# Causal masking of diagonal score blocks: from an addition on VectorE to an accumulated matmul

## The chip, the cores and the metric

The kernel runs on one core of one Trainium2 chip. The metric is the time of one execution on the device in microseconds (us). Where engines are named, PE is TensorE, DVE is VectorE, ACT is ScalarE, POOL is GpSimd and SP is SyncE.

## The reference

Input X is 4 sequences of 2048 tokens with 256 channels, in float32. Four residual blocks follow one another, each after a layer norm: attention A, a feed-forward block with token shift, attention B, and the same feed-forward block again. Cut to the attention, which is what the change touches:

```
# block A: 16 heads of 16 channels
scores = einsum('bhqk,bhsk->bhqs', q, k) * scale
scores = where(tril(ones(S, S)), scores, -inf)      # key s <= query q
attn_out = einsum('bhqs,bhsk->bhqk', softmax(scores), v)

# block B: 16 heads of 16 channels; q is k moved by one token, k and v are normalised
att = einsum('bhqd,bhkd->bhqk', q, k)
att = where(t[None, :] <= t[:T - 1, None], att, -inf)
y = einsum('bhqk,bhkd->bhqd', softmax(att), v)      # row 0 is zero

x = x + A(ln(x));  x = x + ffn(ln(x));  x = x + B(ln(x));  x = x + ffn(ln(x))
```

## The kernel before

**Stages.** A loop over the 4 sequences runs, for each, the projections of block A, `attend("A")`, a feed-forward stage, the projections of block B, `attend("B")` and the second feed-forward stage. So there are 8 attentions. Each engine has its own program, and the programs meet at semaphores.

**An attention.** The 16 heads are taken 4 at a time (`HG`), so an attention has 4 instances, and the whole kernel 32. They run in a loop of two passes (`Fori(0, NHG // 2)`); each pass holds two instances that are written out, `u` = 0 and `u` = 1. There are thus three places in an attention where one instance follows another: `u` 0 to 1 in the first pass, the loop's jump back (`u` 1 to 0), and `u` 0 to 1 in the second pass. Where an instance begins, `begin` (line 898) reads flags and, where a head's scores could be large, runs `row_maxima`; otherwise it branches past that code.

**Banks and groups.** Scores are computed transposed, with 128 keys on the partitions and up to 512 queries on the free axis. A unit is one key block of 128 against one query chunk of 512 (or the part of the chunk that isn't masked wholly) for one head. `score_banks` (line 68) packs units into banks of 512 columns. Query chunk `qc` has 4*`qc` key blocks ahead of the diagonal, each a full bank for each of the 4 heads, and then the diagonal blocks: block `d` with 512 columns, `d+1` with 384 and `d+3` with 128 in one bank, two heads' `d+2` with 256 each in one bank. `GROUPS` pairs the banks; an instance has 69 groups, and 21 of them are diagonal (6 in the first chunk, 5 in each of the other three). A diagonal bank holds one or two units, and the first 128 columns of each unit are the block in which the triangular mask falls. Counted over an instance these are 16 units for each chunk, 64 in all.

**The pipeline.** PE computes the scores of group `gi + 3` (line 932, bf16, 99 contraction rows) and then the value products of group `gi` (line 950, float32). ACT takes the exponential of a group, 1024 columns in one instruction (line 661), from PSUM into `probs` in SBUF. PSUM has three score buffers of two banks (`NS_BUF`), so the scores of group `gi + 3` wait for the exponential of group `gi`; there are six buffers of `probs`. On diagonal groups DVE first adds the mask tile `mask_kq` in PSUM (`masks`, line 1344), 128 columns for each unit, one instruction for each group, and ACT waits for that (`masked`) and not for the scores.

**What else DVE does there.** DVE works through its own program in order: the masks of the chunk's groups, then `take` (line 1360, it copies a finished output chunk out of PSUM), `normalise` (line 1366), and the next chunk's masks. At an instance's end it runs the first three masks of the next instance (`ahead`, line 1382), then `take` of the last chunk, then the jump back where the loop turns, and then the other masks of chunk 0. In the last instance of an attention `first_residual` (line 1309), with a layer norm, stands ahead of the masks of chunk 3. PE's `turn` (line 956) transposes what `take` copied.

**Other names.** `row_maxima` on PE (line 830) already holds an accumulated matmul of `ident_b` and a mask tile (line 846), for query-major scores. `probs` names a semaphore as well as the tile: it counts exponentials. `stage` holds the keys and queries, in bf16 parts, that lines 932 and 843 read.

Of the kernel before, what the change touches and what calls it, by code (L numbers as in the profile page):

```python
# [28 lines left out]
ALU = mybir.AluOpType  # L29
AX_X = mybir.AxisListType.X  # L30

P = 128
# [4 lines left out]
CH = 512  # L37
NCH = S // CH
TB = CH // P
HG = 4  # L40
NHG = H // HG
# [42 lines left out]
GB = 2  # L84
NS_BUF = 3
# [3 lines left out]
GROUPS = [BANKS[0:1], BANKS[1:2]] + [BANKS[i:i + GB] for i in range(2, len(BANKS), GB)]  # L89
NG = len(GROUPS)  # L90
# [61 lines left out]
def hybrid_kernel(nc, t, out):  # L152
    with ExitStack() as ctx:
# [183 lines left out]
        for a in "AB":  # L337
            att[a] = {n: sem(f"{n}_{a}") for n in (
                "kq0", "kq1", *(f"kq_first{c}" for c in range(NCH)), "scores", "probs", "p_free", "vst",
                "masked", "o_ev", "o_T", "o_free", "o_step", "mx_scores", "mx_used", "mx_col", "mx_T", "mx_step", "mx_row",  # L340
                "mx_dma")}

        def held(eng):
# [262 lines left out]
        def _(act):  # L606
# [41 lines left out]
            def attend(a, b, g, left_used):  # L648
                sm = att[a]
                for u in range(2):  # L650
                    inst = b * NHG + g * 2 + u
                    for gi, grp in enumerate(GROUPS):
                        if u == 0 and gi == NP_BUF - 2:
                            act.wait_ge(*left_used)
                        if gi in DIAG_GROUPS:
                            act.wait_ge(sm["masked"], inst * ND + DIAG_GROUPS.index(gi) + 1)
                        else:
                            act.wait_ge(sm["scores"], inst * NG + gi + 1)
                        act.wait_ge(sm["p_free"], P_FREE_0 + inst * NG + gi + 1 - NP_BUF)
                        w = len(grp) * CH  # L660
                        nc.scalar.activation(  # L661
                            probs[:, (u * NG + gi) % NP_BUF, 0:w],
                            ps[:, GB * (gi % NS_BUF):GB * (gi % NS_BUF) + len(grp), :].rearrange("p a n -> p (a n)"),
                            ACT.Exp, scale=SCALE[a]).then_inc(sm["probs"], 1)
                        if u == 1 and gi - 2 in FIRST_O + FIRST_LN:
                            with act.If(g > NHG // 2 - 2):
                                first_copy(b, "AB".index(a), gi - 2)
# [107 lines left out]
        def _(pe):  # L775
# [116 lines left out]
            def attend(a, b):  # L892
# [29 lines left out]
                def scores(u, inst, gi, fresh=False):  # L922
                    kk = stage[0:KROWS, 2 * u, :].rearrange("r (j n) -> r j n", j=HG)
                    qq = stage[0:KROWS, 2 * u + 1, :].rearrange("r (j n) -> r j n", j=HG)
                    if not fresh:
                        pe.wait_ge(sm["probs"], inst * NG + gi + 1 - NS_BUF)
                    if u == 0 and GROUPS[gi][0][0][0] != GROUPS[gi - 1][0][0][0] and gi:
                        first_there(GROUPS[gi][0][0][0])
                    for n, bk in enumerate(GROUPS[gi]):
                        for qc, kb, j, q0, w, col in bk:  # L930
                            o = ps[:, GB * (gi % NS_BUF) + n, col:col + w]
                            last = pe.matmul(o, kk[:, j, kb * P:(kb + 1) * P],  # L932
                                             qq[:, j, qc * CH + q0:qc * CH + q0 + w], start=True, stop=True)
                    last.then_inc(sm["scores"], 1)

                def products(u, inst, gi):
# [250 lines left out]
        def _(dve):  # L1187
# [86 lines left out]
            with dve.Fori(0, B) as b:  # L1274
# [46 lines left out]
                def attend(a):  # L1321
# [19 lines left out]
                            dve.sem_inc(sm["mx_step"], 3 * HG)  # L1341
                            dve.sem_inc(sm["mx_row"], HG)

                    def masks(hg, groups):

                        inst = b * NHG + hg
                        for gi, at, n in groups:
                            dve.wait_ge(sm["scores"], inst * NG + gi + 1)
                            bk = GB * (gi % NS_BUF)
                            nb = len(GROUPS[gi])  # L1350
                            units = ps[:, bk:bk + nb, :]
                            if n == 1:
                                units = units[:, :, 0:P]
                                mask = mask_kq[a][:, :].unsqueeze(1).to_broadcast([P, nb, P])
                            else:
                                units = units.rearrange("p b (n w) -> p b n w", w=P)[:, :, 0:at // P + 1:at // P, :]
                                mask = mask_kq[a][:, :].unsqueeze(1).unsqueeze(1).to_broadcast([P, nb, n, P])
                            nc.vector.tensor_tensor(units, units, mask, ALU.add).then_inc(sm["masked"], 1)  # L1358

                    def take(hg, qc):  # L1360
                        inst = b * NHG + hg

# [19 lines left out]
                    def ahead(hg):  # L1382

                        begin(hg)
                        masks(hg, DIAG[0][:NS_BUF])

                    ahead(0)
                    with dve.Fori(0, NHG // 2) as g:
                        for u in range(2):
                            hg = g * 2 + u  # L1390
                            masks(hg, DIAG[0][NS_BUF:])
                            if u == 1:
                                normalise(hg - 1, NCH - 1)
                            else:
# [2 lines left out]
                            for qc in range(NCH - 1):  # L1397
                                take(hg, qc)
                                normalise(hg, qc)
                                if u == 1 and qc == NCH - 2:  # L1400
                                    with dve.If(g > NHG // 2 - 2):
                                        first_residual("AB".index(a))
                                masks(hg, DIAG[qc + 1])

                            if u == 0:
                                ahead(hg + 1)
# [213 lines left out]
```

## Time and profile before

| | |
|---|---|
| Time, median of 3 runs | 3817.01 us |
| Lowest and highest run | 3812.78 and 3830.15 us |
| Span of the profiled execution, first to last instruction | 3815.5 us |
| PE busy | 3341.0 us, 88% of the span |
| ACT busy | 2521.1 us, 66% |
| DVE busy | 1584.7 us, 42% |
| Mean granted TensorE clock | 0.923 of full speed |
| Exponentials (line 661) | 2208 of 1019 ns |
| Mask additions (line 1358) | 672 in all, 369.3 us busy |

The profiled execution has no time of its own in the profile beside its span; the span is 1.5 us under the median of the runs. Busy time of a PE matmul is modelled from its start to its estimated end and overlaps the next one, so where matmuls follow each other their starts are what tells the pace.

### The profile page before, as it was taken

The numbers are of one execution on the slowest core, as the hardware profiler recorded it, in microseconds if no ns is written. First come the engines' busy times: TensorE is split into PE (matmuls) and PEld (weight loads), VectorE is DVE, ScalarE is ACT, GpSimd is POOL, SyncE is SP. The second block draws the span as 40 slices with busy tenths as digits, with TensorE's granted clock in tenths as the row PEclk, the third lists the DMA queues.
The fourth block names the chain that finished last, engine by engine and source line by source line (L and its number), as shares of the span: only waits on it lengthen the run. The fifth ranks groups of instructions, "written<-read, shape, count | busy, mean of one in ns | idle before, by whom it ended". The sixth has DMA issues, their size and how long they took to land.

```text
span 3815.5 us, 60575 instructions
## 1 busy us (share of the span) xinstructions
PE 3341.0 (88%) x19930; PEld 1358.3 (36%) x19931; DVE 1584.7 (42%) x3607; ACT 2521.1 (66%) x2786; POOL 380.6 (10%) x384
## 2 busy tenths in 40 slices
PE   6999859989899985998989998599898999959988
PEld 4222532225422353222542236222263223622225
DVE  4222682235522278223552227722464212862146
ACT  4888348865488834886459882588636887258853
POOL 4000130001200013000120001300012000120001
PEclk8999979989899997998999999799899999979989
DMA  5420024200432002320053200332015220042200
GB/s 146 74 38 2 1 62 76 36 2 24 129 65 37 2 1 73 65 36 2 23 138 56 36 2 1 87 51 36 2 33 148 36 36 2 1 101 37 36 2 23
DMA packets 96168, 167.82 MB, mean 44 GB/s; under 512 B 10442, under 2 KB 90826, under 8 KB 90826
## 3 DMA queue, kind: packets, MB, share of 16 engines
q1 hardware_dynamic: 95632, 161.14, 19.6%
q8 instruction: 279, 4.57, 0.5%
q14 instruction: 257, 2.11, 0.2%
HBM read 114.82 MB, written 46.24 MB: 42 GB/s over the span
## 4 chain that ended last, share of the span: by engine, by line
PE 70%; DVE 16%; issue 9%; ACT 3%; POOL 1%; DMA 1%; SPq 1%; DVEq 0%; ACTq 0%; POOLq 0%
PE ps L950 29%; PE ps L932 28%; PE ps L826 4%; PE ps L818 3%; PE ps L960 2%; PE ps L803 2%; ACT probs L661 1%; DVE nw_u L1217 1%; DVE nw_u L1219 1%; DVE stage L1421 1%; DVE nw_y L1221 1%; DVE ln_st L1227 1%; DVE stage L1239 1%; DVE pmax L1292 1%; PE ps L868 1%
## 5 line engine op out<-in xcount | busy, mean ns | idle before, releaser
L661 ACT ACTIVATE probs<-ps 128x1024 f32<-128x1024 f32 (+1 forms) x2208 | 2083.7, 1019 | 469.8 <-DVE ps L1358 378.0
L932 PE MATMUL ps<-stage 99*128 99x512 bf16 (+3 forms) x5120 | 1206.9, 362 | 139.9 <-issue 104.4
L950 PE MATMUL ps<-probs,v_st 128*32 128x512 f32 (+3 forms) x10240 | 1215.0, 556 | 4.6 <-issue 4.6
L932 PEld LDWEIGHTS ps<-stage 99*128 99x128 bf16 x5120 | 407.1, 100 | 1150.0 <-ACT probs L661 593.3
L950 PEld LDWEIGHTS ps<-probs,v_st 128*32 128x32 f32 x10240 | 222.3, 111 | 517.7 <-issue 264.6
L1358 DVE TENSOR_TENSOR ps<-ps,mask_kq_B 128x512 f32<-128x512 f32 (+2 forms) x336 | 184.4, 570 | 525.7 <-PE ps L932 522.6
L1358 DVE TENSOR_TENSOR ps<-ps,mask_kq_A 128x512 f32<-128x512 f32 (+2 forms) x336 | 184.9, 570 | 523.4 <-PE ps L932 519.3
L818 PE MATMUL ps<-stage,wT 128*128 128x512 f32 x512 | 233.4, 606 | 12.3 <-DVE stage L1462 7.7
L826 PE MATMUL ps<-wT,stage 128*128 128x256 f32 x1024 | 235.2, 385 | 2.7 <-DVE x_res L1450 2.7
L1364 DVE COPY o_ev<-ps 128x512 f32<-128x512 f32 x128 | 88.5, 692 | 339.2 <-PE ps L950 339.2
L555 POOL TENSOR_TENSOR stage<-xnT 128x512 f32<-128x512 f32 x64 | 65.0, 1037 | 1530.2 <-ACT xnT L646 1327.6
L826 PEld LDWEIGHTS ps<-wT,stage 128*128 128x128 f32 x1024 | 196.6, 194 | 44.3 <-issue 19.7
L1371 DVE TENSOR_SCALAR den<-ps 128x16 f32<-128x16 f32 x128 | 22.4, 175 | 401.5 <-PE ps L960 401.5
L709 ACT ACTIVATE stage<-ps 128x1024 f32<-128x1024 f32 x32 | 32.7, 1023 | 230.1 <-PE ps L818 230.1
L542 POOL COPY v_st<-v_all 128x256 f32 x128 | 45.2, 400 | 1242.8 <-PE ps L950 1240.2
L818 PEld LDWEIGHTS ps<-stage,wT 128*128 128x128 f32 x512 | 98.0, 195 | 123.6 <-issue 104.3
L621 ACT COPY stage<-ps 128x1024 f32<-128x1024 f32 x48 | 48.7, 1014 | 131.5 <-PE ps L818 117.5
L818 PE MATMUL ps<-xnT,wT 128*128 128x512 f32 x256 | 118.1, 615 | 4.4 <-ACT xnT L621 4.4
L1462 DVE SCALAR_TENSOR_TENSOR stage<-stage,mu,xnT 128x512 f32<-128x512 f32 x64 | 63.3, 1027 | 80.8 <-POOL stage L555 80.8
L1227 DVE BATCH_NORM_STATS2 ln_st<-x_res 128x6 f32<-128x256 f32 x256 | 89.7, 412 | 15.8 <-DMA x_res<-in_L_attn_a_X 13.5
L803 PE MATMUL ps<-ident,stage 128*128 128x128 f32 x320 | 48.9, 302 | 53.8 <-DVE stage L1239 52.6
L826 PE MATMUL ps<-wT,probs 128*128 128x256 f32 x384 | 88.1, 383 | 6.5 <-ACT probs L621 6.5
(154 smaller groups left out, 2501.5 us busy)
## 6 DMA issues: line engine op xcount, KB each, us to landing
stage<-part_a SPq DMA_DIRECT2D x36, 512.0 KB
stage<-part_b SPq DMA_DIRECT2D x36, 512.0 KB
part_a<-probs SPq DMA_DIRECT2D x96, 128.0 KB
part_a<-last_parts SPq DMA_DIRECT2D x96, 128.0 KB
stage<-part_a SPq DMA_DIRECT2D x12, 768.0 KB
stage<-part_a SPq DMA_DIRECT2D x36, 256.0 KB
stage<-part_b SPq DMA_DIRECT2D x12, 768.0 KB
stage<-part_b SPq DMA_DIRECT2D x36, 256.0 KB
```

The source lines that it names most:

```text
L555: pool.tensor_tensor(x_diff[:, kt, :], now[:, kt, :], before[:, kt, :], ALU.subtract).then_inc(s_diff, 1)
L661: nc.scalar.activation(probs[:, (u * NG + gi) % NP_BUF, 0:w], ps[:, GB * (gi % NS_BUF):GB * (gi % NS_BUF) + len(grp), :].rearrange("p a n ...
L803: last = pe.transpose(ps[:, bk + kt, tb * P:(tb + 1) * P], src[:, tb, kt * P:(kt + 1) * P], ident[:, :])
L818: last = pe.matmul(ps[:, bk, :], wT[:, w, kt, m * P:(m + 1) * P], src[:, kt, :], start=(kt == 0), stop=(kt == KT - 1))
L826: last = pe.matmul(tok_bank(bk, tb), src[:, kt, tb * P:(tb + 1) * P], wT[:, w, kt, :], start=(kt == 0), stop=(kt == KT - 1))
L932: last = pe.matmul(o, kk[:, j, kb * P:(kb + 1) * P], qq[:, j, qc * CH + q0:qc * CH + q0 + w], start=True, stop=True)
L950: last = pe.matmul(ps[HS * j:HS * (j + 1), 6 + qc % 2, q0:q0 + w], v_st[:, u, kb, j, :], probs[:, slot, at:at + w], start=(kb == 0), stop= ...
L960: last = pe.transpose(ps[:, 6 + qc % 2, tb * P:(tb + 1) * P], o_ev[:, qc % 2, tb * P:(tb + 1) * P], ident[:, :])
L1227: step(nc.vector.bn_stats(ln_st[:, tb, :], x_res[:, TB * c + tb, :]))
L1358: nc.vector.tensor_tensor(units, units, mask, ALU.add).then_inc(sm["masked"], 1)
L1364: nc.vector.tensor_copy(o_ev[:, qc % 2, :], ps[:, 6 + qc % 2, :]).then_inc(sm["o_ev"], 1)
L1462: last = nc.vector.scalar_tensor_tensor(x_k[:, kt, :], x_diff[:, kt, :], mu[:, 1, kt:kt + 1], before[:, kt, :], ALU.mult, ALU.add)
```

## The change

DVE no longer adds the mask. On a diagonal unit PE issues, right behind the score matmul, a second one that multiplies the 128x128 bf16 identity `ident_b` (as weights) with the 128x128 bf16 mask tile and accumulates the product onto the first 128 columns of the unit. ACT waits for the scores on every group; the semaphore `masked` and the function `masks` are gone.

```
@@ PE, scores @@
                         for qc, kb, j, q0, w, col in bk:
                             o = ps[:, GB * (gi % NS_BUF) + n, col:col + w]
+                            diagonal = kb >= TB * qc
                             last = pe.matmul(o, kk[:, j, kb * P:(kb + 1) * P],
-                                             qq[:, j, qc * CH + q0:qc * CH + q0 + w], start=True, stop=True)
+                                             qq[:, j, qc * CH + q0:qc * CH + q0 + w], start=True, stop=not diagonal,
+                                             skip_group_check=diagonal)
+                            if diagonal:
+                                last = pe.matmul(o[:, 0:P], ident_b[:, :], mask_kq[a][:, :], start=False, stop=True,
+                                                 skip_group_check=True)
@@ ACT, attend @@
-                        if gi in DIAG_GROUPS:
-                            act.wait_ge(sm["masked"], inst * ND + DIAG_GROUPS.index(gi) + 1)
-                        else:
-                            act.wait_ge(sm["scores"], inst * NG + gi + 1)
+                        act.wait_ge(sm["scores"], inst * NG + gi + 1)
@@ DVE, attend @@
-                    def masks(hg, groups):
...
-                        masks(hg, DIAG[0][:NS_BUF])
...
-                            masks(hg, DIAG[0][NS_BUF:])
...
-                                masks(hg, DIAG[qc + 1])
```

The first place is PE's program in the middle of an instance, where the diagonal groups of chunk 1 begin. A row is one or several equal instructions with the line, the tiles and the size; a register row stands ahead of a group and belongs to its wait. Before:

```order
L932 MATMUL ps<-stage 128x384
L932 MATMUL ps<-stage 128x128
L932 MATMUL ps<-stage 128x384
L932 MATMUL ps<-stage 128x128
L950 MATMUL ps<-probs,v_st 32x512 x4
```

And in the changed kernel, at the same place:

```order
L930 MATMUL ps<-stage 128x384
L934 MATMUL ps<-mask_kq_A,ident_b 128x128
L930 MATMUL ps<-stage 128x128
L934 MATMUL ps<-mask_kq_A,ident_b 128x128
L930 MATMUL ps<-stage 128x384
L934 MATMUL ps<-mask_kq_A,ident_b 128x128
L930 MATMUL ps<-stage 128x128
L934 MATMUL ps<-mask_kq_A,ident_b 128x128
L952 MATMUL ps<-probs,v_st 32x512 x4
```

Four matmuls of one group have become eight, and the value products stand behind them as they did.

The second place is DVE's program at the head of the attention's loop, where the jump back lands (the row of line 1388) and chunk 0's other masks and the normalisation of the instance before follow. Before:

```order
L1388 UNCONDITIONAL_BRANCH
L1388 ISA
L1358 TENSOR_TENSOR ps<-ps,mask_kq_A 128x2x2x128
L1348 REGISTER_ALU
L1358 TENSOR_TENSOR ps<-ps,mask_kq_A 128x2x2x128
L1348 REGISTER_ALU
L1358 TENSOR_TENSOR ps<-ps,mask_kq_A 128x4x128
L1395 COMPARE_AND_BRANCH
L1371 TENSOR_SCALAR den<-ps 128x16
```

In the changed kernel the rows of line 1358 are gone from there and from everywhere else; the normalisation follows the jump directly.

## Rows read from the trace of the kernel before

**Rows 1.** The page: span, busy time, and the chain's shares by line

```profile
span 3815.5 us, 60575 instructions
...
PE 3341.0 (88%) x19930; PEld 1358.3 (36%) x19931; DVE 1584.7 (42%) x3607; ACT 2521.1 (66%) x2786; POOL 380.6 (10%) x384
...
PE ps L950 29%; PE ps L932 28%; PE ps L826 4%; PE ps L818 3%; PE ps L960 2%; PE ps L803 2%; ACT probs L661 1%; DVE nw_u L1217 1%; DVE nw_u L1219 1%; DVE stage L1421 1%; DVE nw_y L1221 1%; DVE ln_st L1227 1%; DVE stage L1239 1%; DVE pmax L1292 1%; PE ps L868 1%
```

**Rows 2.** Busy time inside one instance: window, length, then engines, clock, DMA

```profile
172.00:238.00 66.00, 66.00 (x460) 19.63 (x457) 15.21 (x33) 60.91 (x65) 1.31 (x4) 0.99 0.30 51
```

**Rows 3.** ACT's waits for masks (sum, times, longest); the page on line 1358

```profile
ACT probs L661 <- DVE ps L1358: 378.0, 265, 30.1
...
L1358 DVE TENSOR_TENSOR ps<-ps,mask_kq_B 128x512 f32<-128x512 f32 (+2 forms) x336 | 184.4, 570 | 525.7 <-PE ps L932 522.6
```

**Rows 4.** Timeline, PE, off the diagonal: start us, length us, what, [idle before]

```profile
200.03 1.04 PE L932 MATMUL ps<-stage 99*128 99x512 bf16 x4
...
200.99 1.06 PE L950 MATMUL ps<-probs,v_st 128*32 128x512 f32 x8
```

**Rows 5.** Timeline, all engines, diagonal groups of chunk 1 of one instance

```profile
186.50 1.05 PE L932 MATMUL ps<-stage 99*128 99x384 bf16 x8
...
187.47 1.07 PE L950 MATMUL ps<-probs,v_st 128*32 128x512 f32 x8
187.96 8.36 ACT L661 ACTIVATE probs<-ps 128x1024 f32<-128x1024 f32 x9 [0.30 <-DVE ps L1358]
...
188.47 1.17 PE L932 MATMUL ps<-stage 99*128 99x512 bf16 x4
...
189.57 1.07 PE L950 MATMUL ps<-probs,v_st 128*32 128x384 f32 x16
```

**Rows 6.** Timeline in very short windows, PE: starts of short matmuls and their successors

```profile
186.89 0.44 PE L932 MATMUL ps<-stage 99*128 99x128 bf16 x3
...
186.94 0.38 PE L932 MATMUL ps<-stage 99*128 99x256 bf16 x2
...
801.46 0.22 PE L843 MATMUL ps<-stage 99*128 99x128 bf16 x1
801.51 0.22 PE L846 MATMUL ps<-mask_qk_B,ident_b 128*128 128x128 bf16 x1
...
797.15 0.31 PE L846 MATMUL ps<-mask_qk_B,ident_b 128*128 128x128 bf16 x1
797.26 0.64 PE L843 MATMUL ps<-stage 99*128 99x512 bf16 x1
```

**Rows 7.** Timeline, PE and ACT, where instance 1 follows instance 0

```profile
162.71 1.07 PE L950 MATMUL ps<-probs,v_st 128*32 128x512 f32 x8
163.19 1.94 ACT L661 ACTIVATE probs<-ps 128x1024 f32<-128x1024 f32 x2 [0.30 <-DVE ps L1358]
...
166.70 1.03 PE L932 MATMUL ps<-stage 99*128 99x512 bf16 x2 [2.92 <-issue]
...
171.51 2.19 PE L932 MATMUL ps<-stage 99*128 99x384 bf16 x12
```

**Rows 8.** Timeline, all engines, behind the loop's jump in an attention B

```profile
723.84 1.07 PE L950 MATMUL ps<-probs,v_st 128*32 128x512 f32 x8
725.30 1.89 DVE L1358 TENSOR_TENSOR ps<-ps,mask_kq_B 128x512 f32<-128x512 f32 x3 [2.33 <-issue]
726.11 6.52 ACT L661 ACTIVATE probs<-ps 128x1024 f32<-128x1024 f32 x7 [3.31 <-DVE ps L1358]
...
727.27 0.60 PE L932 MATMUL ps<-stage 99*128 99x512 bf16 x2 [2.36 <-ACT probs L661]
```

**Rows 9.** Timeline, PE: waits behind the loop's jump (first, last), B's start

```profile
252.80 0.60 PE L932 MATMUL ps<-stage 99*128 99x512 bf16 x2 [0.80 <-ACT probs L661]
...
568.31 2.74 PE L932 MATMUL ps<-stage 99*128 99x384 bf16 x12 [1.62 <-ACT probs L661]
...
3563.89 0.60 PE L932 MATMUL ps<-stage 99*128 99x512 bf16 x2 [0.86 <-ACT probs L661]
```

More of the change, by code:

```diff
@@ L339, in hybrid_kernel @@
                 "kq0", "kq1", *(f"kq_first{c}" for c in range(NCH)), "scores", "probs", "p_free", "vst",
-                "masked", "o_ev", "o_T", "o_free", "o_step", "mx_scores", "mx_used", "mx_col", "mx_T", "mx_step", "mx_row",
+                "o_ev", "o_T", "o_free", "o_step", "mx_scores", "mx_used", "mx_col", "mx_T", "mx_step", "mx_row",
                 "mx_dma")}
@@ L1342, in begin @@
                             dve.sem_inc(sm["mx_row"], HG)
-                    def masks(hg, groups):
[L1346 to L1358, printed above, removed]
                     def take(hg, qc):
```

## The prediction

> **What bounds the kernel now.** I read the page first, and on it the chain of work that ended last rather than the busy shares [rows 1]. The value products and the scores, both PE's, hold 29% and 28% of the span; the exponential has 1% and the mask addition is not among the lines named. Then I looked at the busy time inside an instance: in a stretch of 66 us PE is busy for all 66.00, at a clock of 0.99, and ACT for 60.91 [rows 2]. PE's busy time is modelled, so I checked the pace by starts. Off the diagonal, the four scores of two groups start at 200.03 and the eight products at 200.99 [rows 4], with the next scores at 201.99: some 1.965 us for two groups, 0.98 each. ACT needs 8.36 us for nine exponentials in a row [rows 5], 0.93 each. So inside an instance PE sets the pace, and ACT has 0.05 us of room in each group.
>
> The view of the waits seems to say something else: ACT waited 378.0 us for masks, 265 times [rows 3]. The question that decides this case is how much of that reaches PE. On the diagonal of chunk 1 ACT waits 0.30 us for a mask just before 187.96, but PE goes on: scores at 186.50, products at 187.47, scores at 188.47, which is the usual step of 0.97 and 1.00 [rows 5]. Only the batch at 188.47 takes 1.10 us to the next products at 189.57, where 0.97 is usual. The late masks have cost PE 0.13 us. ACT, being the faster of the two, wins the rest back itself.
>
> **What is added.** 64 matmuls of 128 columns for each instance, by 32 instances: 2048, with as many weight loads. This kind stands in the trace already, in other places. A score matmul of 128 columns at 186.89 is followed at 186.94 by the next; one at 801.46 is followed by the identity-and-mask matmul at 801.51 [rows 6]. The printed starts are 0.05 apart, and 0.06 at another such pair in the same group; I take 0.055 us. The weight load is in this: each of these has weights of its own, and the group with four more loads than a plain one also took 0.97 us from 186.50 to 187.47 [rows 5]. So 2048 x 0.055 = 112.6 us. They stand in PE's stream between two things that PE would do at once, so they are on the path wherever PE doesn't wait.
>
> At the lower clock the same matmul takes 0.11 us (797.15 to 797.26) [rows 6]. That matters at the head of an instance: PE restarts after a gap of 2.92 us at 166.70, and two 512-column scores are busy for 1.03 us there [rows 7] where the same two take 0.60 us elsewhere [rows 9]: the 1.2 GHz level. The twelve scores at 171.51, 3072 columns, take 2.19 us [rows 7], between the 1.28 us of 2.4 GHz and the 2.56 us of 1.2 GHz; the clock rises among them. If it rises at the same moment after the restart as before, the work that is pushed behind it runs at full speed and the added matmuls cost 0.055 us after all. If it rises after the same amount of work, some 10 of the 16 at a head cost 0.11: 32 heads x 10 x 0.055 = 18 us more. No row decides between the two; I take the first, since PE is busy all the same with the added work in it, and keep 18 us for the range.
>
> A rule speaks for a higher price. Rows first: 0.055 us from one 128-column matmul to the next, loads included [rows 6]. The Trainium skill, page "TensorE: Matmul & The Clock Gate", section "Back-to-back issue gap", gives about 81 ns for each 128-column matmul in a sustained stream of load and matmul pairs, and some 56 ns only without the loads. By that figure the added work would be 166 us. The trace does not agree so far, but it never shows more than two such short matmuls in a row, and the change makes three in a row in a bank that has a 384 and a 128 unit.
>
> **What is taken away.** DVE loses 672 instructions, of which one half is busy for 184.4 us [rows 3]. DVE has time to spare there (15.21 of 66 us busy [rows 2]), so that is worth nothing in itself. What counts is where PE waited for an exponential that waited for a mask:
> - Mid-instance, 0.13 us at the last diagonal groups of chunks 1 and 2: 0.26 x 32 = 8.3 us. Gone, since the scores are ready before ACT is. Next late is PE itself.
> - Behind the loop's jump DVE comes to its first mask only at 725.30, after 2.33 us of issue with no work; the exponential follows at 726.11 and PE's scores at 727.27, after 2.36 us of idling [rows 8]. In the changed kernel ACT needs only the scores, which PE began at 722.35. The eight attentions have one such wait each, 0.80 in the first and 0.86 in the last [rows 9]; the eight are 0.80, 2.36, 0.74, 1.12, 2.11, 0.38, 0.91 and 0.86, and one has 0.81 more just ahead: 10.1 us. All of it goes; the added matmuls fill the place.
> - At the start of each attention B, PE waits for the first exponentials (1.62 us in the first, with ACT's table load in it [rows 9]; 6.1 us over the four). The mask is about half of that; the load stays. 3 us.
>
> Sum: 21.4 us saved. What is not touched is PE's gap at each instance's head, 2.92 us of issue in `begin` [rows 7].
>
> **The sum.** 3815.5 + 112.6 - 21.4 = 3906.7 us of span. The median of the runs lies 1.5 us over the span, so 3908 us, 2.4% slower.
>
> **Rivals.**
> - The mask really is the limit (faster). The mechanism: in diagonal groups the round of score, mask, exponential and next score through three buffers sets the pace, and taking 0.4 to 0.7 us of DVE out of each round shortens it. Were all 378.0 us of ACT's waits on the path, the time would be 3815.5 - 378 + 112.6 = 3550 us. The point from which this wins is a mask wait of PE over 0.055 x 2048 / 672 = 0.17 us for each diagonal group. The rows show 0.13 us for five groups [rows 5]. 3%.
> - The work is hidden (no change). PE would have to wait 0.9 us in each diagonal chunk; it does so only behind the loop. At the best, the 2.92 us at every head [rows 7] swallow part, and 3815 to 3835 us result. 4%.
> - The head of an instance hangs on ACT. The gap ends at 166.70, 1.6 us after ACT's last exponential of the instance, which began in the pair at 163.19 after a wait for a mask [rows 7]. If that is a cause (and not, as I read the program, two things at a fixed distance from the products at 162.71), then the four last masks' added 0.9 us is paid back by the mask's own 0.8 us that no longer stand ahead of ACT, at 24 places in all: 21 us less, 3887 us. 13%.
> - Short matmuls in a row cost more than the pairs show. With 0.081 us for each, the sum would be 3817 + 166 - 21 = 3962 us. That figure is the page's named above; from rows alone the upper bound is the same spacing at the lower clock, 0.11 us for all, 225 us and 4021 us. I hold it possible for a part of them: 10%, around 3945 to 3965 us.
>
> **Chances and range.** The forecast has 70%, from 3895 to 3935 us: its upper end is with the 18 us for the clock and half of the savings, its lower end with 0.053 us for each (128 columns at 2.4 GHz) and a few us more saved at the heads. The rival with the head has 13%, the dear short matmuls 10%, hidden 4%, faster 3%. The range for 8 in 10 is 3878 to 3945 us: all of the first two but for their tails, and it leaves out the dear matmuls, the hidden and the faster case. A measurement of this kernel can tell about 0.5% (19 us) from no change. Slower by more: 0.93; within: 0.04; faster: 0.03.
>
> **What would show it.** In the profile after, PE should have 2048 matmuls at the new line and the spacing behind each 128-column one should read 0.05 to 0.06 us; 0.08 would be the dear case. A batch of scores with four masks in two groups should go from 0.97 to 1.19 us, with eight to 1.41. ACT should wait for scores, more often than before inside the diagonal, and PE should not wait for it there. Behind the loop's jump PE's wait of 0.4 to 2.4 us should be gone. The distance from the last full products of an instance to the first scores of the next (3.99 us, from 162.71 to 166.70) should stay; if it shrinks to about 3.1, the third rival was right. PE's share of the chain should rise over 70%. I would be wrong if PE's gaps of issue at the heads change with the longer program, for which the trace of before has no row.

## The result, and the profile of the changed kernel

The changed kernel takes 3912.35 us (median of 4 runs, 3907.22 to 3926.56) against 3817.25 us before: a ratio of 1.0255, with a 95% interval from 1.0237 to 1.0273. That is 95.1 us slower; 3908 us had been forecast. The profiled execution has a span of 3909.0 us, 93.5 us over that of [rows 1].

The page of the changed kernel: span, busy time, the chain's shares by engine and line, and the groups of the new line 934.

```profile
span 3909.0 us, 63355 instructions
...
PE 3431.2 (88%) x21978; PEld 1496.8 (38%) x21979; DVE 1216.6 (31%) x2935; ACT 2558.8 (65%) x2786; POOL 381.2 (10%) x384
...
PE 70%; DVE 15%; issue 10%; ACT 2%; POOL 1%; DMA 1%; SPq 1%; DVEq 0%; ACTq 0%; POOLq 0%
...
L930 PE MATMUL ps<-stage 99*128 99x512 bf16 (+3 forms) x5120 | 1293.8, 358 | 152.4 <-issue 128.7
...
L934 PE MATMUL ps<-mask_kq_B,ident_b 128*128 128x128 bf16 x1024 | 200.1, 232 | 0.0
L934 PE MATMUL ps<-mask_kq_A,ident_b 128*128 128x128 bf16 x1024 | 195.9, 229 | 0.0
```

PE has the 2048 added matmuls, DVE has lost its 672 additions and 368.1 us of busy time; neither number says what the change costs. The busy time of one added matmul, 0.23 us, is no price: it overlaps its neighbours. The starts of the matmuls give the price. Here is PE's timeline of the changed kernel at the diagonal of chunk 1, the place of [rows 5] (start us, length us, what).

```profile
186.75 0.39 PE L930 MATMUL ps<-stage 99*128 99x512 bf16 x1
...
187.53 0.22 PE L930 MATMUL ps<-stage 99*128 99x128 bf16 x1
187.59 0.22 PE L934 MATMUL ps<-mask_kq_A,ident_b 128*128 128x128 bf16 x1
187.65 0.33 PE L930 MATMUL ps<-stage 99*128 99x384 bf16 x1
...
188.08 1.06 PE L952 MATMUL ps<-probs,v_st 128*32 128x512 f32 x8
189.08 0.34 PE L930 MATMUL ps<-stage 99*128 99x384 bf16 x1
...
190.54 1.06 PE L952 MATMUL ps<-probs,v_st 128*32 128x512 f32 x8
191.54 1.04 PE L930 MATMUL ps<-stage 99*128 99x512 bf16 x4
192.51 1.07 PE L952 MATMUL ps<-probs,v_st 128*32 128x384 f32 x16
```

From the mask's matmul at 187.59 to the next at 187.65 are 0.06 us, with short matmuls before and behind it. The batch at 186.75 has six masks and lasts 1.33 us to the products at 188.08; the one at 189.08 has eight and lasts 1.46, where [rows 5] had 0.97. The next, at 191.54, lasts 0.97; in [rows 5] the batch there lasted 1.10, since it waited for a late mask. So a chunk pays 16 x 0.06 = 0.96 us and gets 0.13 back.

To see where the rest went I took, in every trace, the start of DVE's `den` instruction: there is one for each output chunk, 128 in all, so 127 intervals can be set side by side. 64 of them lie wholly inside an instance (two for each), and each is 0.82 to 0.84 us longer than before, 53.2 us together. The others, at the places where instances and stages meet, make up the other 40. They aren't alike: those with the loop's jump in B grew by 34.2 us over the four sequences (7.22, 7.55, 10.7, 8.7) and the ones behind them by 5.6, while the jump in A gave 0.9 back. The rest moved by up to 8.4 us each way in the sum over the sequences and nearly cancels. The four intervals in B are a surprise. PE's timeline of the changed kernel there, with the idle time ahead of an instruction in brackets ("issue" is idle time in which the engine waited for nothing that the profile shows):

```profile
731.32 1.08 PE L952 MATMUL ps<-probs,v_st 128*32 128x256 f32 x8
734.07 0.50 PE L930 MATMUL ps<-stage 99*128 99x384 bf16 x1 [1.67 <-issue]
...
738.02 1.94 PE L952 MATMUL ps<-probs,v_st 128*32 128x512 f32 x8
744.10 1.01 PE L930 MATMUL ps<-stage 99*128 99x512 bf16 x2 [4.15 <-issue]
```

At 738.02 the products run, and then PE stands for 4.15 us without waiting for any engine; in the three other sequences it is 4.42, 6.03 and 5.63 us. The kernel before has no gap of issue there; it waited 2.36 us for an exponential [rows 8]. The busy times of that stretch in the changed kernel (columns as in [rows 2]):

```profile
741.00:744.00 3.00, 0.00 (x0) 0.00 (x0) 0.00 (x0) 0.00 (x0) 0.00 (x0) 0.88 1.07 164
```

No engine computes for 3 us, and the DMA engines are full (share 1.07, 164 GB/s). They carry the next instance's keys and queries, which SP has issued from 732.71 on. The view of the DMA queues for 739 to 744.2 tells what else is among them:

```profile
DMA packets 96, 0.93 MB, mean 178 GB/s; under 512 B 39, under 2 KB 39, under 8 KB 39
...
q1 hardware_dynamic: 94, 0.90, 101.4%
q8 instruction: 1, 0.02, 1.6%
q14 instruction: 1, 0.01, 1.0%
```

Two packets of instructions travel among 94 of data; the one on queue 8 is of 16 KiB. So I had two things to settle: whether the two prices of the sum, for the matmul and for the masks on DVE, were right, and what these gaps are.

### The profile page after: what moved, and what is told of

It is laid out like the page before. It is cut to its first block, busy times and chain, and to the rows that moved or that the text cites. A ratio compares the mean times of both kernels' runs of the same rounds, so it can differ in the third digit from the quotient of the medians.

```text
span 3909.0 us, 63355 instructions
## 1 busy us (share of the span) xinstructions
PE 3431.2 (88%) x21978; PEld 1496.8 (38%) x21979; DVE 1216.6 (31%) x2935; ACT 2558.8 (65%) x2786; POOL 381.2 (10%) x384
## 3 DMA queue, kind: packets, MB, share of 16 engines
q14 instruction: 249, 2.04, 0.2%
## 4 chain that ended last, share of the span: by engine, by line
PE 70%; DVE 15%; issue 10%; ACT 2%; POOL 1%; DMA 1%; SPq 1%; DVEq 0%; ACTq 0%; POOLq 0%
PE ps L930 28%; PE ps L952 28%; PE ps L934 3%; PE ps L823 3%; PE ps L815 3%; PE ps L962 2%; DVE nw_y L1223 1%; DVE stage L1404 1%; DVE nw_u L1221 1%; ACT probs L658 1%; PE ps L800 1%; DVE nw_u L1219 1%; DVE ln_st L1229 1%; DVE stage L1241 1%; DVE pmax L1294 1%
## 5 line engine op out<-in xcount | busy, mean ns | idle before, releaser
L658 ACT ACTIVATE probs<-ps 128x1024 f32<-128x1024 f32 (+1 forms) x2208 | 2121.5, 1011 | 522.4 <-PE ps L934 356.9
L930 PE MATMUL ps<-stage 99*128 99x512 bf16 (+3 forms) x5120 | 1293.8, 358 | 152.4 <-issue 128.7
L952 PE MATMUL ps<-probs,v_st 128*32 128x512 f32 (+3 forms) x10240 | 1202.7, 553 | 0.0
L930 PEld LDWEIGHTS ps<-stage 99*128 99x128 bf16 x5120 | 450.0, 100 | 1146.8 <-ACT probs L658 665.2
L934 PE MATMUL ps<-mask_kq_B,ident_b 128*128 128x128 bf16 x1024 | 200.1, 232 | 0.0
L934 PE MATMUL ps<-mask_kq_A,ident_b 128*128 128x128 bf16 x1024 | 195.9, 229 | 0.0
L706 ACT ACTIVATE stage<-ps 128x1024 f32<-128x1024 f32 x32 | 32.8, 1024 | 229.3 <-PE ps L815 229.3
L1294 DVE TENSOR_REDUCE pmax<-ps 128x1 f32<-128x1024 f32 (+4 forms) x96 | 79.7, 910 | 99.6 <-PE ps L843 99.5
L934 PEld LDWEIGHTS ps<-mask_kq_B,ident_b 128*128 128x128 bf16 x1024 | 106.6, 104 | 5.7
L934 PEld LDWEIGHTS ps<-mask_kq_A,ident_b 128*128 128x128 bf16 x1024 | 104.8, 102 | 5.7
```

Source lines behind the costliest of these rows:

```text
L658: nc.scalar.activation(probs[:, (u * NG + gi) % NP_BUF, 0:w], ps[:, GB * (gi % NS_BUF):GB * (gi % NS_BUF) + len(grp), :].rearrange("p a n ...
L930: last = pe.matmul(o, kk[:, j, kb * P:(kb + 1) * P], qq[:, j, qc * CH + q0:qc * CH + q0 + w], start=True, stop=not diagonal, skip_group_ch ...
L934: last = pe.matmul(o[:, 0:P], ident_b[:, :], mask_kq[a][:, :], start=False, stop=True, skip_group_check=True)
L952: last = pe.matmul(ps[HS * j:HS * (j + 1), 6 + qc % 2, q0:q0 + w], v_st[:, u, kb, j, :], probs[:, slot, at:at + w], start=(kb == 0), stop= ...
L1294: nc.vector.tensor_reduce(pmax[:, 1 if b0 else 0, qb:qb + 1], src, AX_X, ALU.max).then_inc(sm["mx_used"], 1)
```

## Experiments

### The masks twice, and no masks

The first kernel is the changed one with DVE's additions left in, the second the one before without them. In the second the exponential's scale is also multiplied by 1e-30, so that unmasked scores stay finite, and its output is not the reference's.

```
 e1_both, on the kernel before: PE's scores as in the changed kernel
+                            if diagonal:
+                                last = pe.matmul(o[:, 0:P], ident_b[:, :], mask_kq[a][:, :], start=False, ...)

 e2_neither, on the kernel before: ACT and DVE
-                            act.wait_ge(sm["masked"], inst * ND + DIAG_GROUPS.index(gi) + 1)
+                        act.wait_ge(sm["scores"], inst * NG + gi + 1)
...
-                            nc.vector.tensor_tensor(units, units, mask, ALU.add).then_inc(sm["masked"], 1)
```

> PE's program is that of the changed kernel (2048 identity-and-mask matmuls), DVE's and ACT's programs are those of before: the mask is added twice, once on PE and once on DVE, which gives the same result. Theory 1 (the change is the added PE work less the waits for DVE's masks): all of the PE work stays, none of the waits goes, so it is slower than the changed kernel by what the waits were worth, 20 to 35 us: 3930 to 3948 us. Rival (the waits were worth nothing, ACT merely waited beside PE): 3912 us. On the new PE gaps of 4 to 6 us of issue behind the loop's jump in each attention B: if they come from where PE's instructions lie, they are here too, since PE's program is the same; if they come from DVE and ACT running ahead with no masks, they are gone and 35 us with them.

> No mask at all on the scores of the attention, neither on PE nor on DVE (the exponential's scale is 1e-30 so that unmasked scores stay finite; the output is not the reference's). PE's program is that of before. Theory 1: before less the waits for masks, 3817 - 21 (my forecast's sum) to - 35, so 3782 to 3796 us; the added matmuls then cost 3912 less this, 116 to 130 us, 0.057 to 0.063 each. Rival (the waits were worth nothing): 3817 us. The new gaps in attention B: none if they come from where PE's instructions lie; four of 4 to 6 us if they come from the missing masks on DVE.

With both masks: 3928.73 us (3924.13 to 3935.31), ratio 1.0291 (1.0259 to 1.0323). The 64 intervals inside instances are +53.2 us, the same as with PE's masks alone: beside the added matmuls DVE's additions no longer reach PE there. Between instances they still cost 16.4 us by the medians and 20.1 by the spans; the intervals of the two ratios overlap, so the size is loose, and 3928.73 us lies just under the range that was expected. The gaps in B stay (+35.7 us in the four intervals), so DVE's masks have nothing to do with them.

With none: 3773.85 us (3769.22 to 3779.63), ratio 0.989 (0.9861 to 0.992), 41.6 us faster than the kernel before beside it and faster than expected; by spans 48.2, where the profiled execution is the fastest of the four. B's jump has no new gap here (-1.8 us in the four intervals). Inside the instances it gained 8.5 us, 0.12 to 0.14 for each, where the prediction had 0.26 for each two. Elsewhere it gained 39.7 us, where the prediction had 13.1. The page's row for the scores of this kernel, to be set against 1206.9 us busy and 139.9 us idle (104.4 of issue, 16.2 waiting for ACT) of the same row before:

```profile
L929 PE MATMUL ps<-stage 99*128 99x512 bf16 (+3 forms) x5120 | 1190.0, 360 | 122.5 <-issue 96.7
```

PE idles 17.4 us less and takes 16.9 us less for the same matmuls (8.5 of it is the 0.13 us inside instances). So without masks on PE DVE's additions were worth 40 to 48 us, not 21. Beside PE's masks, as e1_both has them, they were worth only 16 to 20: the added matmuls partly fill the same waits, so what "DVE's masks cost" depends on the order in which the two edits are made. Part of the 40 to 48 us is no wait for a mask at all: 7.7 us are issue, and the largest terms lie where one instance follows another (A's second pass 8.8 us, A's jump 6.5, from B to the next sequence 9.4). Which of it is DVE's order and which the changed place of DVE's code, this run can't tell.

### Moving PE's code

The gaps come in B only, whose program is as A's but lies elsewhere. So I put matmuls that are never executed ahead of B's loop in PE's program, in a branch that isn't taken; each is two instructions.

```
 e3_pad64, e4_pad128, e5_pad192, e6_pad256: on the changed kernel, n = 32, 64, 96, 128;
 e7_before_pad128: on the kernel before, n = 64
+                        if fresh and a == "B":
+                            for _ in range(n):
+                                pe.matmul(ps[:, 0, 0:P], ident_b[:, :], mask_kq[a][:, :], start=True, stop=True)
```

> The changed kernel with 32 matmuls (64 instructions with their weight loads) put into PE's program in a branch of attention B that is never taken, ahead of its loop: they don't run, but everything of PE behind them lies 64 instructions later. Theory 1 for the gaps (they come from where instructions lie): the interval in attention B from the last output chunk of instance 1 to the first of instance 2, 43 to 46 us in the changed kernel against 36 before, changes by 2 us or more, and the time by four times that. Rival (they come from the stream of events): interval and time stay, 3912 us within 5.

> As the kernel with 32 unexecuted matmuls, but with 64 (128 instructions). Theory 1: the interval differs from the unpadded kernel, and from the one with 32, by 2 us or more in at least one of the two; if both gaps vanish the time is about 3872 us. Rival: 3912 us within 5.

> The changed kernel with 96 unexecuted matmuls (192 instructions) ahead of attention B's loop in PE's program. Only intervals of attention B may move if place is what counts. Theory (place of PE's instructions, with some period): the intervals at instance ends of B differ again from those with 0, 64 and 128 instructions, each by up to 9 us, and the time lies between 3870 and 3925 us. Rival (chance variation from run to run): B's intervals scatter around those of the changed kernel.

> As before, with 128 unexecuted matmuls (256 instructions). The Trainium skill, page 'Runtime: NRT & Kernel Launch', section 'Instruction fetch mechanics', has an engine's instructions fetched in blocks of 256. If place counts with that period, the intervals of attention B come back to those of the changed kernel: +34 us over before in the four loop intervals, within 6, and 3912 us within 8. If place counts without that period, they don't come back, and the loop intervals' sum is anywhere between 0 and 40 us.

> The kernel before with the same 64 unexecuted matmuls (128 instructions) ahead of attention B's loop. Theory (place of PE's instructions): the kernel before moves too, by 3 us or more, though no executed instruction differs; the direction is open, 3790 to 3850 us. Rival (only the changed kernel, without masks on DVE, is sensitive): 3815 us within 3.

| instructions put in | time, us | ratio to before, 95% | B's jump intervals against before, us |
|---|---|---|---|
| 0 (changed kernel) | 3912.35 | 1.0237 to 1.0273 | +34.2 |
| 64 | 3924.70 | 1.0245 to 1.0307 | +30.0 |
| 128 | 3894.72 | 1.0157 to 1.0224 | +3.4 |
| 192 | 3898.61 | 1.0183 to 1.0231 | -0.8 |
| 256 | 3918.52 | 1.0252 to 1.0286 | +28.6 |
| 128, kernel before | 3800.61 | 0.9932 to 0.9965 | -0.5 |

Code that never runs moves the time by 30 us, and 256 instructions bring the pattern of 0 back. The place moves stalls about rather than removing them: with 192 B's jump lost 35.0 us against the changed kernel and the time only 13.7, since the intervals behind the jump now stand at +10.9 us and those of the instance after at +9.8; with 128 the time came to 3894.72 us and not to the 3872 expected. With 64 the jump intervals changed by 0.6 to 2.8 us only, against the 2 us or more that were expected, and the time rose by 12.4 us, with ratios whose intervals overlap. With 64 the gap stands at another instruction, between a score and its mask. PE's timelines of e3_pad64 and then of e6_pad256:

```profile
735.71 0.27 PE L937 MATMUL ps<-mask_kq_B,ident_b 128*128 128x128 bf16 x1 [2.72 <-issue]
```

```profile
737.80 1.01 PE L933 MATMUL ps<-stage 99*128 99x512 bf16 x2 [4.03 <-issue]
```

So the gap hangs on the place of the code, with a period that 256 instructions fit. The Trainium skill, page "Runtime: NRT & Kernel Launch", section "Instruction fetch mechanics", says that instructions are fetched in blocks of 16 KiB, 256 of them, over a DMA queue of the engine's own. The traces agree with the 256, and with the 16 KiB of each packet on queue 8. It also calls the cost of crossing a block "mostly hidden"; the 4.15 us above are not.

The same padding makes the kernel before faster too, by 0.5%. Side by side with 128 instructions in both, the change costs 94.1 us, near the 95.1 without. That is no proof of the change's own cost: in this pair neither kernel has the gap in B's jump, but B's first interval between instances is 9.5 us shorter than in the kernel before in the one and 7.5 longer in the other.

### An edit of DVE's order that went wrong

If DVE's masks between instances cost so much, moving them might help. In e8_early_masks DVE does the next instance's remaining masks of chunk 0 ahead of the loop's jump.

```
 e8_early_masks, on the kernel before, DVE
                     ahead(0)
+                    masks(0, DIAG[0][NS_BUF:])
                     with dve.Fori(0, NHG // 2) as g:
...
-                            masks(hg, DIAG[0][NS_BUF:])
...
                             take(hg, NCH - 1)
+                            if u == 0:
+                                masks(hg + 1, DIAG[0][NS_BUF:])
+                            else:
+                                with dve.If(g < NHG // 2 - 1):
+                                    masks(at_most(hg + 1, NHG - 1), DIAG[0][NS_BUF:])
```

> The kernel before, PE's and ACT's programs untouched, with DVE's masks of chunk 0's last three groups moved ahead of the loop's jump, behind the copy of the last output chunk, so that DVE's jump no longer stands ahead of them. Theory (behind the jump DVE's late first mask holds ACT, and ACT holds PE): the waits of PE for ACT behind the jump go, 9 to 10 us over the eight attentions, 3815 to about 3805 us. Rival (PE's own stall behind the jump is what ends last there): 3815 us. A risk: normalise now stands behind these masks, which costs nothing since it waits for a transpose that comes later.

It took 3866.45 us (3860.03 to 3877.08), ratio 1.0122 (1.0102 to 1.0141): 50 us slower, not faster. The timeline of this kernel at A's jump, DVE and PE:

```profile
251.63 0.70 DVE L1358 TENSOR_TENSOR ps<-ps,mask_kq_A 128x512 f32<-128x512 f32 x1 [0.15 <-PE ps L932]
263.77 0.17 DVE L1371 TENSOR_SCALAR den<-ps 128x16 f32<-128x16 f32 x1 [11.44 <-issue]
```

```profile
264.83 1.94 PE L950 MATMUL ps<-probs,v_st 128*32 128x512 f32 x8 [7.37 <-DVE o_tok L1377]
```

DVE's jump back took 11.44 us, and PE waited 7.37 us for what came behind it; in the eight attentions the jump took 6.30 to 11.89 us. In the kernel before, the jump was made between 248.06 and the mask at 250.83, beginning 0.44 us behind the first of SP's seven loads (issued from 247.62 to 251.73); here it began at 252.33, when SP had issued all of them, from 247.74 on. (The expectation of e11_late_early puts the jump of the kernel before ahead of the loads; the rows don't.) Its windows show full DMA engines again (last but one column):

```profile
257.00:260.00 3.00, 0.47 (x3) 0.00 (x0) 0.00 (x0) 2.00 (x3) 0.00 (x0) 0.87 1.01 142
260.00:263.00 3.00, 0.00 (x0) 0.00 (x0) 0.00 (x0) 0.00 (x0) 0.00 (x0) 0.50 0.90 134
```

If this reading is right, it is not DVE's order that costs but its timing: an instruction fetch that comes behind the loads waits among them, on DVE as on PE. Full DMA engines alone aren't enough: in the kernel before their share is already 1.11 from 248 to 249, during the jump of 2.77 us. The reading can be tried by moving the loads.

### Moving the loads

SP now waits, before it issues an instance's key and query loads, until PE is 16 groups into the instance before. No other engine's program changes.

```
 e9_late_after on the changed kernel, e10_late_before on the one before, e11_late_early on e8_early_masks
             def load_group(a, u, hg, inst):
                 sp.wait_ge(att[a]["p_free"], (inst + 1) * NG)
                 held(sp)
+                sp.wait_ge(att[a]["scores"], (inst - 1) * NG + 16)
+                held(sp)
```

> The changed kernel, with SP issuing each instance's key and query loads only once PE has begun the 16th score group of the instance before it, instead of as soon as the probabilities' buffers are free. In the changed kernel PE stands still for 4.15 to 6.03 us at four places behind the loop's jump in B, while the DMA engines are full with these loads. Theory (code fetch and loads share the DMA engines): these stalls shrink to about the 2 to 3 us that such a place has without loads beside it, B's loop intervals lose 25 to 40 us, and the time is 3865 to 3885 us. Rival (the fetch takes this long wherever the loads lie, so it is the place of the code alone): B's loop intervals stay within 5 us, and the time is 3905 to 3915 us. Other rival (the loads collide with the fetches of the next jump instead): the gaps move to another interval and the time is 3900 to 3925 us.

> The kernel before with the same later issue of the loads and nothing else. Its trace has no stall of over 3 us behind B's jump, so theory expects little: 3795 to 3815 us, since only the gaps of 2 to 3 us at the jumps and crossings can shrink. Rival (the loads cost nothing where they were): 3812 to 3820 us. A time above 3830 us would say that the loads now collide with something in the middle of an instance.

> The kernel before with DVE's first masks of the next instance moved ahead of the loop's jump, as in the run that took 3866.45 us, and with the later issue of the loads. There DVE's jump stood for 11.44 us within the loads, where it took 2.8 us before they began. Theory: with the loads elsewhere the jump takes 2 to 4 us again, A's loop loses its 30 us and B's its 35, and the time is 3795 to 3815 us. Rival (DVE's order alone is what costs, for instance because its den rows wait behind the masks): the time stays at 3855 to 3875 us.

| kernel | loads as they were | loads later | ratio to before of the latter, 95% |
|---|---|---|---|
| changed | 3912.35 | 3879.64 | 1.0146 to 1.0180 |
| before | 3817.25 | 3812.53 | 0.9983 to 1.0000 |
| before, masks ahead of the jump | 3866.45 | 3801.26 | 0.9958 to 0.9982 |

The theory's ranges held for all three (that of e10_late_before overlaps with its rival's, so it tells only that nothing new collides). Where a fetch had met the loads the move is worth 33 and 65 us; in the kernel before, where PE and DVE had no such stall, about 4, which is not clear of nothing. In the changed kernel the gap of 4.15 us is gone; PE's timeline of e9_late_after at that place, and its windows:

```profile
734.66 0.50 PE L932 MATMUL ps<-stage 99*128 99x384 bf16 x1 [2.38 <-issue]
...
738.61 1.69 PE L954 MATMUL ps<-probs,v_st 128*32 128x512 f32 x8
740.23 0.60 PE L932 MATMUL ps<-stage 99*128 99x512 bf16 x2
```

```profile
738.00:741.00 3.00, 3.00 (x18) 1.04 (x16) 0.00 (x0) 1.61 (x3) 0.00 (x0) 0.68 0.02 5
741.00:744.00 3.00, 3.00 (x33) 1.03 (x32) 0.97 (x4) 2.53 (x3) 0.00 (x0) 1.00 0.00 0
```

PE is busy for all of both windows. Instruction packets still travel, now alone; the DMA queues of e9_late_after from 738 to 741:

```profile
q8 instruction: 1, 0.02, 2.0%
```

So the same kind of fetch is hidden with idle DMA engines and costs 4 to 6 us among the loads. What the runs show is that the stall needs both, the code's place and the loads.

That PE waits for such a packet is inferred from the packets' times, which say more than the windows. Queue 8 carries 290 packets of 16 KiB in both kernels, so the same one can be followed. The 54th travels from 735.16 to 736.09 in e9_late_after, and PE works on through 740.23 with no gap. In the changed kernel it travels from 741.04 to 742.40, behind the loads, and PE goes on at 744.10, 1.70 us after it landed. That distance recurs: of the 38 gaps of issue over 2.5 us in the changed kernel 34 end 1.56 to 2.04 us after a packet of queue 8. In e8_early_masks a packet of queue 14 travels from 260.96 to 261.82, and DVE goes on 1.95 us later; in e11_late_early it does so at 248.22. The packets themselves take 0.8 to 1.8 us even among the loads; the rest of a stall lies ahead of the packet's start. What holds it there the profile doesn't show.

Not all fetches are hidden without loads: the gap ahead of 734.66 is even longer than in the changed kernel (2.38 us, 1.67 there), with a packet of queue 8 that lands at 733.04 and idle DMA engines. And the DVE jump of e8_early_masks, in e11_late_early:

```profile
246.24 1.90 DVE L1360 TENSOR_TENSOR ps<-ps,mask_kq_A 128x512 f32<-128x512 f32 x3 [0.83 <-PE ps L934]
...
250.16 0.17 DVE L1373 TENSOR_SCALAR den<-ps 128x16 f32<-128x16 f32 x1 [2.02 <-PE ps L962]
```

From the end of the masks (248.14) to `den` are 2.02 us instead of 11.44, and `den` waited for PE at the end, so the jump takes no more. In the eight attentions it is 2.01 to 2.99 us. The masks ahead of the jump now gain 11 us over e10_late_before.

With the loads out of the way the change costs 3879.64 - 3812.53 = 67.1 us by the medians, 76.5 by the spans. From the parts it should be 122.9 - 48.2 = 74.7 us by the spans (2048 matmuls of 0.06, less what e2_neither gained), but 122.9 - 41.6 = 81.3 by the medians. So the parts add up only within some 14 us, and the places of the code, which differ between the two kernels, are in it too.

### What is left of the code's place

The last kernel is e11_late_early with the 128 instructions of e7_before_pad128, to see if the place matters when no loads are near.

> The kernel of e11_late_early (masks on DVE, the next instance's first masks ahead of the loop's jump, loads 16 groups into the instance) with the 128 instructions that are never executed ahead of B's loop on PE, as in e7_before_pad128. If the code's place costs only where its fetches meet the loads, it is worth next to nothing now that the loads lie elsewhere: 3795 to 3808 us, within 6 us of the 3801.26 us without the padding. If a place costs whether or not loads run beside it, the padding is worth here what it was worth in the kernel before, 10 to 16 us: 3785 to 3792 us.

It took 3779.58 us (3775.32 to 3789.03), ratio 0.9907 (0.989 to 0.9923): 21.7 us less than without the padding, though its profiled execution, the slowest of the four, shows only 6.1 us. Of the two cases the second came, and by more than its 10 to 16 us: the place costs even without loads. The intervals from B's first instance to its second gave 8.7 us of it; the same intervals are 9.5 us shorter in e7_before_pad128 than in the kernel before. One gap there, in PE's timelines of e11_late_early and then of e12_late_early_pad128:

```profile
790.10 0.23 PE L845 MATMUL ps<-stage 99*128 99x128 bf16 x1 [4.49 <-issue]
```

```profile
787.88 0.23 PE L845 MATMUL ps<-stage 99*128 99x128 bf16 x1 [3.33 <-issue]
```

Why this place is the better one the traces don't show. It is also the fastest kernel of the study that computes the reference's result, 0.9% under the one before, with masks on DVE.

## Why the forecast held, and what of it did not

**The total was right by luck: errors of both signs cancelled.** In spans:

| | forecast | measured |
|---|---|---|
| 2048 added matmuls | +112.6 | +122.9 (0.06 us each) |
| DVE's masks, inside instances | -8.3 | -8.3 (0.13 us each; e2_neither 8.5) |
| DVE's masks, between instances | -13.1 | -39.7 (e2_neither; 33.1 by the medians) |
| fetches among the loads, B's jump | 0 | +30.9 (what e9_late_after took away: 25.3 + 5.6) |
| left over | | -12.3 |
| sum | +91.2 | +93.5 |

The left-over 12.3 us is no measured term. The places of all later code changed, and the change of one and the same interval between instances differs by up to 3.5 us among the four sequences of one trace. Nor is the split the only one: with PE's masks put in first the steps are +113.3 us (e1_both against before, its gaps in B included) and -16.4 (the changed kernel against e1_both).

**The price of a matmul** was taken from printed starts 0.05 and 0.06 apart [rows 6] as 0.055; with the rows of the changed kernel it is 0.06, in sequences of alternating short matmuls too (the 64 intervals inside instances are 61.7 us longer than in e2_neither, for 1024 added matmuls). This is 10.3 us more than the sum had, within its bounds. The rival of dear short matmuls (0.081 us) did not happen.

**What holds PE inside an instance** was read rightly. The 0.13 us at two groups [rows 5] is gone, 0.97 became 1.46 with eight masks (1.41 forecast), and 378.0 us of ACT's waits for masks [rows 3] became waits for scores. The view of the waits of the changed kernel (sum, times, longest):

```profile
ACT probs L658 <- PE ps L934: 356.9, 290, 29.3
```

The rival that saw in those 378.0 us the limit fell by this: the wait stays when DVE's addition goes, and e2_neither, with no mask at all, gained 41.6 us and not 378.

**The savings between instances failed as a term.** The step was the list of eight waits behind the loop's jump (10.1 us) and the start of B (3 us). It counted only places where PE waited for an exponential [rows 8 and 9]. As a count of those it came near: PE's score matmuls waited 16.2 us for exponentials in the kernel before and 5.1 in the changed one. But e2_neither measured 39.7 us against these 13.1, and where the rest lies is not shown; the masks' removal also moves DVE's code. It also supposed that the added matmuls fill the place with no new wait. In A the wait of 0.80 us [rows 9] is gone from its place, but one batch earlier PE now waits 0.97 us for an exponential, at 251.96. In B, in the place of the 2.36 us of [rows 8], stands the gap of 4.15 us, and one batch earlier 1.67 us of issue at 734.07.

**The head hung on nothing of ACT's.** In the changed kernel the last full products stand at 164.94 and the next instance's first scores here:

```profile
164.94 1.06 PE L952 MATMUL ps<-probs,v_st 128*32 128x512 f32 x8
169.14 0.39 PE L930 MATMUL ps<-stage 99*128 99x512 bf16 x1 [3.13 <-issue]
```

The distance is 4.20 us, where [rows 7] had 3.99 and the rival wanted 3.1. It is a gap of issue and doesn't depend on ACT.

**The clock.** The span's mean granted clock is 0.933, and it was 0.923 in the kernel before's profiled execution. The added matmuls alone don't explain this: e1_both has them too and shows 0.927. In the stretch behind B's jump, after a gap, the clock is 0.50 and a mask costs 0.11 us (734.36 to 734.47), as in [rows 6]. The 18 us held for that in the range are not told apart from the rest here.

**The warning that came true.** The prediction named one way to be wrong: gaps of issue that change with the longer program. They did, by 31 us at and behind B's four jumps. The forecast survived because the savings had been put too low by nearly as much (26.6 us by e2_neither). With the loads moved the changed kernel takes 3879.64 us, below the forecast's own range (from 3895) and just inside that for 8 in 10 (from 3878).

## What to carry to other kernels

Moving small work from an idle engine to the one that sets the pace costs its full spacing wherever that engine doesn't wait, however long another engine seemed to wait for the work; ask of a wait not how long it is but whether the pacing engine stood still behind it. In a kernel of long written-out loops, look which DMA loads run while an engine jumps back or shows idle time of issue, and start large loads elsewhere: one added wait on SP's queue took 33 us from one kernel, 65 from another and next to nothing from a third. Before a difference of under 1% is put down to an edit, shift the code with instructions that never run and see whether the difference stays.

## What was not expected of the hardware

- Where an instruction packet came behind full DMA loads PE stood still for 4.15 to 6.03 us and DVE for 6.30 to 11.89 us; with idle DMA engines PE's gap of 4.15 us was gone and DVE's jumps took 2.01 to 2.99 us.
- The packet itself took 0.8 to 1.8 us among the loads, and 34 of PE's 38 longest gaps of issue ended 1.56 to 2.04 us after one had landed.
- Instructions that are never executed, 64 to 256 of them, spread the times of the changed kernel over 30 us, and 256 brought the same pattern back.
- Even without loads near, 128 such instructions were worth 21.7 us. Which gaps this goes to was found only in part (8.7 us between B's first two instances), so the rule for a good place stays open.
